# Eight attention and expert-FFN rounds on one core: low-rank terms as stacked single-pass products instead of folded weights, and the attention rounds written out

## The reference, cut to what matters

```python
x = x + attn(cond(x, itok), W_Q, W_K, W_V, W_o)        # x: (8, 512, 256), 16 heads of 16
x = x + ffn(cond2(x, itok, ...), w1, ..., gate_b)      # 8 experts, the best 2 of each token

def cond2(x, ids, wi, wo, common_*, experts_*):        # D = 256, F = 1024, ranks 16 and 16, ALPHA = 2
    hidden_i  = einsum('bsd,fd->bsf', x, wi)
    hidden_i += ALPHA * einsum('bsr,fr->bsf', einsum('bsd,rd->bsr', x, common_wi_a), common_wi_b)
    hidden_i += _expert_lora(x, ids, experts_wi_a, experts_wi_b)      # the same with matrices of the batch's expert
    hidden_i  = relu(hidden_i)
    hidden_o  = einsum('bsf,df->bsd', hidden_i, wo)
    hidden_o += ALPHA * einsum('bsr,dr->bsd', einsum('bsf,rf->bsr', hidden_i, common_wo_a), common_wo_b)
    hidden_o += _expert_lora(hidden_i, ids, experts_wo_a, experts_wo_b)
    return hidden_o
```

## Time and profile before

| | us |
|---|---|
| three runs | 1587.23, 1591.77, 1601.42 |
| median | 1591.77 |
| the profiled execution, its own time | 1591.71 |
| its span in the trace | 1590.1 |
| round 0, from the start to the first product of round 1 | 111.7 |
| rounds 1 to 7, from the first product of round 1 to that of round 8 | 860.4 |
| round 8, to about 1018 | 46 |
| part B | 572 |

### The profile page before, as it was taken

One profiled execution on the slowest core, in us unless ns is written; L12 is line 12 of the kernel. 1 busy time (PEld: TensorE's weight loads), 2 busy tenths in 40 slices (PEclk: granted clock), 3 DMA queues, 4 the chain that ended last, 5 costly groups with the idle time before them and its releaser, 6 DMA issues.

```text
span 1590.1 us, 34291 instructions
## 1 busy us (share of the span) xinstructions
PE 1460.0 (92%) x10105; PEld 1068.9 (67%) x10106; DVE 912.2 (57%) x1999; ACT 751.6 (47%) x1992; POOL 419.3 (26%) x553
## 2 busy tenths in 40 slices
PE   6999989989999998998999999636989999999997
PEld 3556755765674674674675675634878888888886
DVE  2666655665665664664665666274545555555554
ACT  3665654764663663664564564102333333333332
POOL 2221210211221221121121120032434444445442
PEclk9699989999998998999998997856999999999999
DMA  6121221212212112212221120173453322442221
GB/s 214 63 92 50 90 77 58 74 64 89 74 61 92 59 69 75 78 61 75 69 83 54 58 94 28 57 307 140 110 168 103 84 37 40 142 141 43 36 40 16
DMA packets 46627, 133.74 MB, mean 84 GB/s; under 512 B 9266, under 2 KB 26290, under 8 KB 44722
## 3 DMA queue, kind: packets, MB, share of 16 engines
q0 software_dynamic: 28992, 68.35, 15.8%
q1 hardware_dynamic: 17522, 63.89, 10.9%
HBM read 81.74 MB, written 51.38 MB: 84 GB/s over the span
## 4 chain that ended last, share of the span: by engine, by line
PE 86%; DVE 5%; issue 3%; DMA 2%; ACT 2%; POOL 1%; SPq 0%; POOLq 0%; ACTq 0%; DVEq 0%
PE bank L626 70%; PE bank L773 10%; PE bank L865 4%; PE bank L857 1%; DVE nmax L1181 1%; ACT probs L1014 1%; DMA xg<-hrows,gid 1%; PE bank L781 1%; POOL hit_v L1436 0%; PE bank L733 0%; DVE bank L1119 0%; DVE k_sb L1112 0%; DVE wf_low L1097 0%; ACT hid_high L969 0%; DVE ht_sb L1138 0%
## 5 line engine op out<-in xcount | busy, mean ns | idle before, releaser
L1014 ACT ACTIVATE probs<-bank,nmax 128x512 f32<-128x512 f32 (+3 forms) x512 | 265.4, 524 | 176.8 <-DVE nmax L1181 176.0
L1181 DVE TENSOR_REDUCE nmax<-bank 128x1 f32<-128x512 f32 (+3 forms) x512 | 227.3, 485 | 191.7 <-PE bank L626 190.6
L1416 POOL TENSOR_TENSOR w_rest<-w_rest,w_high 128x512 f32<-128x512 f32 x64 | 81.3, 1271 | 538.8 <-ACT w_high L931 538.8
L1043 ACT ACTIVATE g<-z 128x512 f32<-128x512 f32 x142 | 89.8, 633 | 280.8 <-DVE z L1366 280.8
L773 PE MATMUL bank<-id_f,probs 128*128 128x128 f32 x1280 | 204.9, 291 | 0.3
L626 PE MATMUL bank<-wst,g1t_high 128*128 x568 | 185.6, 408 | 0.9 <-DVE g1t_low L1354 0.9
L773 PEld LDWEIGHTS bank<-id_f,probs 128*128 128x128 f32 x1280 | 136.2, 143 | 48.7 <-issue 26.4
L1458 POOL DMA_INDIRECT out<-y_sb,sid x71 | 114.2, 1609 | 150.4 <-DVE y_sb L1387 68.8
L1195 DVE COPY probs_t<-bank 128x128 f32<-128x128 f32 (+3 forms) x320 | 140.1, 454 | 9.2 <-PE bank L773 9.2
L1366 DVE TENSOR_TENSOR z<-bank,b_sb 128x512 f32<-128x512 f32 x142 | 98.2, 691 | 73.7 <-PE bank L626 48.4
L626 PEld LDWEIGHTS bank<-wst,g1t_high 128*128 128x128 f32 x568 | 102.6, 191 | 20.8 <-issue 1.1
(11 more groups left out here) (171 smaller groups left out, 2885.9 us busy)
## 6 DMA issues: line engine op xcount, KB each, us to landing
wst<-wsplit SPq DMA_DIRECT2D x8, 4096.0 KB, 12.5
w_rest<-in_w_all POOLq DMA_DIRECT2D x64, 256.0 KB, 3.0
wsplit<-w_high POOLq DMA_DIRECT2D x64, 256.0 KB, 2.3
wsplit<-w_rest POOLq DMA_DIRECT2D x64, 256.0 KB, 2.6
hrows<-h_sb SPq DMA_DIRECT2D x8, 528.0 KB, 4.1
x_in<-in_xT SPq DMA_DIRECT2D x8, 512.0 KB, 3.4
x_res<-in_xT SPq DMA_DIRECT2D x8, 512.0 KB, 5.1
out<-x_sb SPq DMA_DIRECT2D x8, 512.0 KB, 3.0
```

The lines of the kernel that those rows point to most:

```text
L1014: taken(nc.scalar.activation(probs[:, s % 4, 0:(i + 1) * P], at(n, rd)[:, 0:(i + 1) * P], ACT.Exp, bias=nmax[:, s % 8:s % 8 + 1], accum_ou ...
L1043: nc.scalar.activation(g[:, :], z[:, :], ACT.Gelu).then_inc(s_g, 1)
L1181: V.tensor_reduce(nmax[:, s % 8:s % 8 + 1], at(n, rd)[:, 0:(s // HEADS + 1) * P], AX.X, ALU.max, negate=True).then_inc(s_max, 1)
L1416: nc.gpsimd.tensor_tensor(w_rest[:, :], w_rest[:, :], w_high[:, :].bitcast(F32), ALU.subtract).then_inc(s_wlow, 1)
```

## The change: stacked low-rank products, and no loop over the rounds

The effective weights are gone. The base weights are split once, in round 0 (eight pieces, `base_piece`: a cast on ScalarE, a subtraction on VectorE, in steps 0 to 8). Each round has, in place of eight folds:

- `low_i`: the 32 low-rank rows of A times x. The 32 rows stand four times in the stationary matrix (`at_cat`: high, high, low, high), so that 128 output rows hold the parts. It is four fp32r products of 512 columns.
- one product more in each `hid`: `wb` (rows 0 to 95 high, rows 96 to 127 low) times `low_i`, 128 rows by 512 columns.
- `low_o`: sixteen fp32r products of 512 columns (eight blocks of F, `hid_high` and `hid_low`), as one filler in step 10. Its result meets `bo` in one product of 256 columns for each of the four `h`.
- `lora_high` on ScalarE (six casts) and `lora_low` on VectorE (four subtractions), which split the matrices of the round's batch, at the head of the round, ahead of everything else that these engines do in it.
- `low_i` and `low_o` each leave their bank by a ScalarE activation of 512 columns and a VectorE operation on 32 rows.

`load_lora` now brings four tensors, 0.8 MB in place of 0.16 MB, and waits for the last `h`. The order of the opening is new. The x1 fillers come one step earlier, in the step that had no filler, and `low_o` takes the place behind them. The loop over rounds 1 to 6 is written out on TensorE, ScalarE, VectorE and SyncE. The core of the diff:

```diff
 FILLERS = ([(("hid", j), k) for j in range(HID_EARLY, KF) for k in range(KD)] +
-           [(None, 0)] + [(("x1", t2), 0) for t2 in range(TB // 2)] +
+           [(("x1", t2), 0) for t2 in range(TB // 2)] + [(("low_o", 0), 0)] +
            [(("h", t), piece) for t in range(TB) for piece in range(H_PIECES)] +
...
     strips = [[(w, g) for w in ("qs", "ks")] for g in range(HC)]
-    qk = [("q", 0), ("k", 0), ("q", 1), ("k", 1)]
     order = [] if feeds else [("cond", o) for o in range(KD)]
-    for n in range(2 * KD):
-        order += [("fold_i", n), qk[n]]
-    dense = [("v", 0), ("v", 1), ("x1t", 0), ("x1t", 1)]
-    for n, ready in enumerate([[], strips[0], strips[1], strips[2] + strips[3]]):
-        order += [dense[n], ("fold_o", n)] + ready
+    order += [("q", 0), ("k", 0), ("x1t", 0), ("x1t", 1), ("q", 1), ("k", 1), ("v", 0)]
+    order += strips[0] + [("low_i", 0)] + strips[1] + [("v", 1)] + strips[2] + strips[3]
     for j in range(HID_EARLY):
         order += [("hid", j)] + strips[4 + j]
...
             def load_lora(e):
-                for r, c in ((R, 0), (3 * R, D + F)):
-                    sp.dma_start(lora[r:r + R, :], lora_e[bass.ds(e, 1), :, c:c + D + F].rearrange("o r n -> (o r) n")
-                                 ).then_inc(s_lora, 16)
+                sp.dma_start(at_raw[:, :, :], lora_at[bass.ds(e, 1), :, :, :].rearrange("o p k r -> (o p) k r")
+                             ).then_inc(s_lora, 16)
+                sp.dma_start(wb_raw[:, :], lora_wb[bass.ds(e, 1), :, :].rearrange("o r n -> (o r) n")
+                             ).then_inc(s_lora, 16)
+                sp.dma_start(ao_raw[:, :, :], lora_ao[bass.ds(e, 1), :, :, :].rearrange("o p k r -> (o p) k r")
+                             ).then_inc(s_lora, 16)
+                sp.dma_start(bo_raw[:, :], lora_bo[bass.ds(e, 1), :, :].rearrange("o r n -> (o r) n")
+                             ).then_inc(s_lora, 16)
 
...
-                        wait_for(rd, full, folds, v_fold)
-                        load_lora(e)
                     wait_for(rd, free, x1s, v_x1)
                     sp.dma_start(out[bass.ds(p, 1), :, :].rearrange("o (t p) d -> p (o t) d", p=P),
                                  x1_sb[:, :, :]).then_inc(s_x1out, 16)
+                    if rd.b is not None:
+                        wait_for(rd, full, hs, v_h)
+                        load_lora(e)
                     sp.wait_ge(s_hdone, v_hdone)
...
-                elif what == "fold_i":
-                    if m == 0:
-                        pe.wait_ge(s_lora, p * 32 + 32)
-                    k, fh = m // 2, m % 2
+                elif what == "low_i":
                     vacant(pe, n, rd)
-                    ins = mm(dst()[:, :], lora[0:2 * R, k * P:(k + 1) * P], lora[0:2 * R, D + fh * 512:D + (fh + 1) * 512],
-                             start=True, stop=True)
-                elif what == "fold_o":
-                    vacant(pe, n, rd)
-                    for u in range(2):
-                        j = 2 * m + u
-                        ins = mm(dst()[:, u * D:(u + 1) * D], lora[2 * R:4 * R, j * P:(j + 1) * P],
-                                 lora[2 * R:4 * R, F:F + D], start=True, stop=True)
+                    pe.wait_ge(s_x_low, p * KD + KD)
+                    pe.wait_ge(s_lora_low, p * LORA_LOWS + 1)
+                    for k in range(KD):
+                        for x in (x_high, x_low):
+                            ins = mm(dst()[:, :], at_cat[:, k, :, :].rearrange("p c r -> p (c r)"), x[:, k, :],
+                                     start=(k == 0 and x is x_high), stop=(k == KD - 1 and x is x_low))
+                elif what == "low_o":
+                    vacant(pe, n, rd, [("hid", j) for j in range(KF)])
+                    pe.wait_ge(s_lora_low, p * LORA_LOWS + 3)
+                    for j in range(KF):
+                        for g in (hid_high, hid_low):
+                            ins = mm(dst()[:, :], ao_cat[:, j, :, :].rearrange("p c r -> p (c r)"), g[:, j, :],
+                                     start=(j == 0 and g is hid_high), stop=(j == KF - 1 and g is hid_low))
                 elif what == "x1t":
                     if m == 0:
...
                         cols = slice(m * P, (m + 1) * P)
                         for w, x in ((wi_high, x_high), (wi_high, x_low), (wi_low, x_high)):
-                            ins = mm(dst()[:, :], w[:, k, cols], x[:, k, :], start=(k == 0 and w is wi_high and x is x_high),
-                                     stop=(k == KD - 1 and w is wi_low))
+                            mm(dst()[:, :], w[:, k, cols], x[:, k, :], start=(k == 0 and w is wi_high and x is x_high),
+                               stop=False)
                     if piece not in (None, KD - 1):
                         return
+                    ins = mm(dst()[:, :], wb[:, m * P:(m + 1) * P], low_i[:, :], start=False, stop=True)
                 elif what == "h":
                     if piece == 0:
-                        vacant(pe, n, rd, ([("fold_o", n4) for n4 in range(KF // 2)] +
-                                           [("hid", j) for j in range(KF)]) if m == 0 else ())
+                        vacant(pe, n, rd, [("hid", j) for j in range(KF)] if m == 0 else ())
...
-                                     stop=(j == KF - 1 and g is hid_low))
+                            mm(dst()[:, 0:D], g[:, j, rows], w[:, j, :],
+                               start=(j == 0 and g is hid_high and w is wf_high), stop=False)
                     if piece < H_PIECES - 1:
                         return
+                    if m == 0:
+                        drained(pe, ("low_o", 0), rd)
+                        pe.wait_ge(s_lora_low, p * LORA_LOWS + LORA_LOWS)
+                    ins = mm(dst()[:, 0:D], low_o[:, m * P:(m + 1) * P], bo[:, :], start=False, stop=True)
                 elif what == "ht":
                     vacant(pe, n, rd, [("h", t) for t in range(TB)] if m == 0 else ())
...
+            pe.wait_ge(s_base_low, BASE_PIECES)
+            for b in range(1, B - 1):
                 turn(Round(b))
             turn(Round(B - 1))
...
-                    act.wait_ge(s_eff, p * FOLDS + (fold_index(n) + 1))
-                    if what == "fold_i":
-                        dst = wi_high[:, m // 2, m % 2 * 512:(m % 2 + 1) * 512]
-                    else:
-                        dst = wf_high[:, 2 * m:2 * m + 2, :].rearrange("p j d -> p (j d)")
-                    nc.scalar.copy(dst, at(n, rd)[:, :]).then_inc(s_eff_high, 1)
+                elif what == "low_i":
+                    filled(act, n, rd)
+                    nc.scalar.activation(low_i[:, :], at(n, rd)[:, :], ACT.Identity, scale=2.0
+                                         ).then_inc(s_low_high, 1)
+                    return
+                elif what == "low_o":
+                    filled(act, n, rd)
+                    nc.scalar.activation(low_o[:, :], at(n, rd)[:, :], ACT.Identity, scale=2.0).then_inc(s_low_high, 1)
                     return
                 elif what == "hid" and piece in (None, KD - 1):
...
+            def lora_high(p):
+                act.wait_ge(s_lora, 16 * LORA_LOADS * (p + 1))
+                nc.scalar.copy(at_cat[:, :, :, :], at_raw[:, :, :].unsqueeze(2).to_broadcast([P, KD, COPIES, RANK])
+                               ).then_inc(s_lora_high, 1)
+                rest = slice(3 * RANK, COPIES * RANK)
+                nc.scalar.copy(wb_top[rest, :], wb_raw[rest, :]).then_inc(s_lora_high, 1)
+                nc.scalar.copy(wb[0:3 * RANK, :], wb_raw[0:3 * RANK, :]).then_inc(s_lora_high, 1)
+                nc.scalar.copy(ao_cat[:, :, :, :], ao_raw[:, :, :].unsqueeze(2).to_broadcast([P, KF, COPIES, RANK])
+                               ).then_inc(s_lora_high, 1)
+                act.wait_ge(s_x1out, p * 16 + 1)
+                nc.scalar.copy(bo_top[rest, :], bo_raw[rest, :]).then_inc(s_lora_high, 1)
+                nc.scalar.copy(bo[0:3 * RANK, :], bo_raw[0:3 * RANK, :]).then_inc(s_lora_high, 1)
+
             def turn(rd):
...
                         cast(b, len(W_OPENING) + W_STEPS.index(step))
+                    if p is None and step < BASE_PIECES:
+                        if step == 0:
+                            act.wait_ge(s_mid, 16 * N_MID)
+                        high, _, raw = base_piece(step)
+                        nc.scalar.copy(high, raw).then_inc(s_base_high, 1)
                     if rt is not None:
...
+            def lora_low(p):
+                rest = slice(3 * RANK, COPIES * RANK)
+                parts_of = ((at_cat[:, :, 2, :], at_raw[:, :, :], at_cat[:, :, 0, :]),
+                            (wb[rest, :], wb_raw[rest, :], wb_top[rest, :]),
+                            (ao_cat[:, :, 2, :], ao_raw[:, :, :], ao_cat[:, :, 0, :]),
+                            (bo[rest, :], bo_raw[rest, :], bo_top[rest, :]))
+                for highs, (low, raw, high) in zip((1, 3, 4, 6), parts_of):
```

(11 more changed lines are left out.)

117 lines of the change are left out of this document (70 added, 47 removed).

## The result

| | before | after |
|---|---|---|
| runs beside each other, us | 1587.23 to 1601.42 (4) | 1536.88 to 1543.16 (4) |
| median | 1590.12 | 1539.83 |
| ratio, 95% interval | | 0.967 [0.962, 0.972] |
| span of the profiled execution | 1590.1 | 1537.3 |
| first product of round 1 | 111.7 | 115.3 |

The change makes the kernel 3.3% faster, 1540 us where 1543 was forecast. The total is near. The page comes first: busy time by engine, and the chain that ended last, by engine (of before: the earlier trace rows).

A forecast was written before the change was run, and what follows sets the result against it. TensorE, busy for 92% of the span, was taken as the bound. Terms of 11.1 + 3.5 + 15.0 + 18.5 + 1.8 - 1.5 = 48.4 us took 1591.8 to 1543 us, range 1524 to 1570.

The forecast's parts named there:

- 1 and 2, products exchanged and the filled step: Rounds 1 to 7: fp32r products replacing eight folds gain 11.1 us; x1 filling step 8's wait for probs gains 3.5.
- 3, loop written out: Ends of rounds 1 to 5: TensorE's five stalls at the jump back go, 15.0 us, with nothing else late there.
- 4, clock at the starts of rounds: Starts of rounds 2 to 7: six falls to 1.2 GHz shorten to about 3.3 us each, a gain of 18.5 us.
- 5, round 8: Round 8: first hid some 12 us in, h at 32.8 us instead of 34.6, a gain of 1.8 us.
- 6, round 0: Round 0's base casts and subtractions cost 1.5 us, bounds 0 and 5.5; low-rank casts at round heads cost nothing.
- the rival that they belong to a round's end: Ends of rounds: queue work, not the jump, causes the 3 us stalls, so they stay; 1558 to 1577 us, chance 0.10.
- the one that straight code starves: Written-out rounds: the program arrives too slowly, TensorE stands about 3.0 us each time; 1616 us at four, chance 0.05.
- The head on ScalarE is covered: Round openings: lora_high's 4.4 us of casts free bank 0 at 7.7 us, 1.9 us before the second k needs it.
- the sum by four passes for true fp32: Folds priced at 0.91 us instead of 1.05: a round gains 0.44 instead of 1.58, the sum 8 us later.
- the row at 400.3: Low-clock window among 128-row products, recovered within 3.3 us; taken as the length of each fall at round starts.
- The rival that the clock doesn't care for rows: Round starts: only TensorE being busy matters, so low-clock pieces stay like the one at 854.2; 1566 us, chance 0.15.
- The rival that it never falls: Round starts: with the stall gone and full products replacing folds, no clock fall remains; 1528 us, chance 0.15.

The follow-up runs named there:

- first experiment: The kernel before with its loop of rounds written out on all four engines, folds kept: 1560.6 us, ratio 0.979.
- second experiment: The changed kernel with rounds 1 to 6 put back into a loop on all four engines: 1550.5 us, ratio 0.974.
- fourth experiment: The kernel before, loop written out, with folds contracting over 128 rows in place of 32 (wrong effective weights): 1530.6 us, ratio 0.961.
- third experiment: The changed kernel with a round's first q waiting only for the next conditioning, not for both filler banks: 1525.9 us, ratio 0.958.
- fifth experiment: The changed kernel with the gate products moved two fillers forward, q's wait for both banks kept: 1518.1 us, ratio 0.954.

## Why the prediction came out right in its total, and which of its steps failed

From the spans, 52.8 us gained in all:

| term | forecast, us | measured, us |
|---|---|---|
| 1 and 2, products exchanged and the filled step | 14.6 | 31.2 (4.46 x 7), of which 7.9 go with the loop alone as well |
| 3, loop written out | 15.0 | 10.5 (15.0 - 6 x 0.75) |
| 4, clock at the starts of rounds | 18.5 | 11 (27 - 16) |
| 5, round 8 | 1.8 | 3.6, with part B, not separable from the clock |
| 6, round 0 | -1.5 | -3.5, not separable |
| sum | 48.4 | 52.8 |

**What held.** TensorE is the bound, and distances between its starts are what products cost (0.23 us, as forecast). The five stalls were the jump's (first experiment: none left; second: back again), which refutes the rival that they belong to a round's end, and the one that straight code starves. The head on ScalarE is covered: its six casts take 4.3 us, 4.4 forecast. Here is one of the three long ones (busy us, then mean ns of one), then the drain that frees bank 0 for the second `k` (ScalarE's timeline):

```profile
L1024 ACT CAST wb<-wb_raw 96x1024 fp32r<-96x1024 f32 x1 | 1.0, 1044 | 0.0
...
233.31 0.57 ACT L974 CAST parts<-bank 128x512 fp32r<-128x512 f32 x1
```

ScalarE has read that bank at 233.9 and VectorE at 234.6; TensorE asks for it at 239.76. Round 8 opened as told: first `hid` at 10.9 us, 12 forecast. Its first `h` comes at 30.6 us where before took 34.6, but that gain is not shown to be the change's: the first experiment, whose round 8 is the old one, has its first `h` at 30.5, with a mean clock of 0.78 in that stretch against 0.65 before.

**Term 1 was too small: the price of a fold.** The step "a `fold_i` takes 112.79 - 111.74 = 1.05 us" counts the fold's own distance. It leaves out that the projection beside it is 0.2 us slower, which was there to be read: in the earlier trace rows q, between two folds, takes 114.70 - 112.79 = 1.91, and in round 0 of the same trace, which has no folds, 21.32 - 19.61 = 1.71:

```profile
19.61 1.88 PE L626 MATMUL bank<-cond,wq_raw 128*128 128x512 f32 x4
21.32 1.88 PE L626 MATMUL bank<-cond,wk_sb 128*128 128x512 f32 x4
```

The fourth experiment gives 1.20 to 1.25 for a fold with its neighbour, eight of them 1.2 to 1.6 us a round more than forecast. The other 1.1 us of the 2.4 by which a round beat its forecast are those that a folded round takes less outside the loop, in the fourth experiment and in the first; no term had them. The forecast also gave the sum by four passes for true fp32, as the Trainium skill (FP8 and Floating Point Precision, TensorE Precision Notes) states. At 128 rows the measurement agrees: 0.86 us is just under four times 0.228. At 32 rows it does not: 1.05 us, and 0.2 beside it.

**Term 3 and the wait that was missed.** "... the first product of the next round, which needs nothing from ScalarE or VectorE but `cond`" is a step that failed. It read q's data and not its code: q waits for two banks, and one is drained by VectorE only after the gate. The fold ahead of q had hidden it. It costs 0.75 us six times, and with the clock 14 us in all (third experiment).

**Term 4 was right in direction and too large.** The six pieces at 1.2 GHz last 6.8 us each, where 3.3 were taken from the row at 400.3. That row had no gap within it; the pieces of the changed kernel have one. Without it the size was right: the falls that are left in the third experiment last 3.4 us. The rival that the clock doesn't care for rows is refuted by the fourth experiment against the first (56 us to 10 with nothing changed but rows and what they hold). The rival that it never falls needed the gap gone and the gate away from the end: that is the fifth experiment, at 1518. Three things are shown, then, to keep the clock down longer or bring it down: 32-row products in the opening, a gap of 0.75 us within the fall, and the order of the last fillers. Most falls set in ahead of q; what starts them is not settled. The Trainium skill (TensorE: Matmul & The Clock Gate, Part 1) draws no line between products by their rows; here the measurement does.

**So the forecast of 1543 is a right sum of wrong parts**: 16.6 us too little in terms 1 and 2, 12 too much in terms 3 and 4. That they cancel to 4 us is luck. Had the gate's drain been read, 1543 would have come out higher, and further from the result.

**What stays open.** Why a 32-row product takes longer than one of 128 rows and slows its neighbour. Why a folded round takes 1.1 us less when it is written out and a stacked one does not. What starts the fall of the clock at a round's end, and why taking out a wait behind its onset makes it rarer. Whether the base pieces cost anything in round 0: kernels with the old round 0 reach round 1 at 111.2, 111.7 and 115.5 us, kernels with the new one at 110.2 to 115.3, and the clock moves both. Why the clock stays low in round 0 for 17 us once and 37 another time with the same code.

## What to carry to other kernels

Before two parts of a change are priced apart, read what the removed instruction covered: the first product of a section hides every wait written ahead of the second, and both its own distance and its neighbour's count as its price. An fp32 product with 32 rows is worth trying with 128 before it is replaced by anything cleverer: the same folds over 128 rows, with the loop written out, took 1531 us, where the new algebra takes 1540. A kernel whose added rows are zeros, so that its results are right, was not measured. Where TensorE is full, a gap is not worth its length but its length and the clock behind it (4.5 us of waiting cost 14 here), so products with few columns, and drains that the next section waits for, belong some steps ahead of a boundary: a new order of five fillers gave 22 us.

## What was not expected of the hardware

- A fold with 128 rows by 512 columns (fp32) took 0.86 us and one with 32 rows 1.05, and the projection of 128 rows next to it 1.72 and 1.92 us.
- With no gap at the starts of rounds, TensorE spent 56 us there at 1.2 GHz with 32-row products among the projections, and 10 us with 128-row ones. With a gap of 0.75 us and no 32-row products it was 41 us, with neither 11, and with wide products at the round's end as well 0.
- The clock was at 1.2 GHz from 226.9 us on, 0.8 us before the gap at the start of round 2 began. Six such falls with the gap inside lasted 6.8 us each; the three that were left when the gap was gone lasted 3.4.
- A folded round took some 115.8 us written out and 116.9 in a loop, beyond the stall at the jump.
- A loop's jump on TensorE cost some 3 us each time (15.0 us in five, the longest 3.1; the longest in the second experiment 3.3).
